# Another order of the work in a quantised feed-forward stage: marks behind products, down product three tiles behind, x standardised by ScalarE

## The reference, cut to what matters

```python
def fp4_quant_dequant(x):             # blocks of 16 along the last dim
    scale = max(max(|xb|) / 6, 1e-12)
    idx = searchsorted(MID, |xb / scale|)
    return GRID[idx] * sign(xb) * scale # grid 0 .5 1 1.5 2 3 4 6
def fp4_linear(x, w):
    return einsum('bsk,nk->bsn', quant(x), quant(w))
h = silu(fp4_linear(x, w_gate)) * fp4_linear(x, w_up)   # 256 -> 704
x = x + fp4_linear(h, w_down)                            # 704 -> 256
```

## Time and profile before

| | us |
|---|---|
| median of 3 runs | 4039.49 |
| profiled execution | 4052.42 |
| its span | 4050.6 |
| PE busy | 3277.3 (81%) |
| DVE busy | 2933.8 (72%) |
| ACT busy | 2218.7 (55%) |
| POOL busy | 1102.7 (27%) |

### The profile page before, as it was taken

The page is one execution under the profiler, slowest core; times in us unless marked ns, Lnnn a source line. Parts: engine busy times, 40 slices in busy tenths (PEclk is TensorE's granted clock), DMA queues, the critical chain, the costliest instruction groups (busy, mean ns, idle before and its releaser), DMA issues. The chain is left out here.

```text
span 4050.6 us, 80801 instructions
## 1 busy us (share of the span) xinstructions
PE 3277.3 (81%) x24792; PEld 2521.1 (62%) x24792; DVE 2933.8 (72%) x7319; ACT 2218.7 (55%) x5224; POOL 1102.7 (27%) x625
## 2 busy tenths in 40 slices
PE   6888887888879469899758888888888886498898
PEld 4666655665656358788635655565556654488787
DVE  4666665666657778888527788787877786589887
ACT  4656665666657323333227777777777775233332
POOL 1000000000000034555322333443334433354554
PEclk9988888899889789999868999899999997799999
DMA  4322323223232010000114334434443432100110
GB/s 82 55 41 37 52 37 52 43 41 48 37 53 32 22 42 16 16 16 16 61 31 63 53 62 67 72 54 65 67 66 59 67 54 46 67 25 27 31 31 26
DMA packets 131686, 185.58 MB, mean 46 GB/s; under 512 B 14102, under 2 KB 79766, under 8 KB 130838
## 3 DMA queue, kind: packets, MB, share of 16 engines
q1 hardware_dynamic: 131526, 183.90, 26.9%
HBM read 45.97 MB, written 28.84 MB: 18 GB/s over the span
## 5 line engine op out<-in xcount | busy, mean ns | idle before, releaser
L368 ACT ACTIVATE a_probs<-a_probs,a_negmax 128x128 f32<-128x128 f32 (+3 forms) x1024 | 569.1, 556 | 463.0 <-DVE a_negmax L291 462.9
L291 DVE CUSTOM_DVE_ANT_0 a_probs<-a_mask,a_score 128x128 f32<-128x128 f32 (+3 forms) x1024 | 487.0, 481 | 279.1 <-PE a_score L438 141.1
L446 PE MATMUL a_turned<-ident,a_probs 128*128 128x128 f32 x2560 | 487.9, 296 | 218.4 <-DVE a_pT L300 203.7
L446 PEld LDWEIGHTS a_turned<-ident,a_probs 128*128 128x128 f32 x2560 | 329.6, 149 | 314.7 <-DVE a_pT L300 213.1
L1023 PE MATMUL f_y_bank<-f_wdT,f_hqT 128*128 128x256 f32 x1536 | 389.0, 407 | 76.4 <-ACT f_hqT L961 76.4
L438 PE MATMUL a_score<-a_stack_k,a_stack_q 112*128 112x128 f32 (+3 forms) x1024 | 439.0, 441 | 0.9 <-DVE a_negmax L291 0.9
L1699 ACT ACTIVATE b_u<-b_u,b_negmax 128x512 f32<-128x512 f32 x512 | 366.5, 716 | 99.5 <-DVE b_negmax L1579 99.1
L1579 DVE CUSTOM_DVE_ANT_0 b_u<-b_u,b_score 128x512 f32<-128x512 f32 x512 | 340.4, 681 | 98.7 <-PE b_score L1825 97.0
L1834 PE MATMUL b_turned<-ident,b_u 128*128 128x128 f32 x2048 | 336.2, 291 | 67.8 <-DVE b_pT L1585 39.8
L1023 PEld LDWEIGHTS f_y_bank<-f_wdT,f_hqT 128*128 128x128 f32 x1536 | 307.3, 205 | 127.7 <-issue 80.9
L1571 DVE SCALAR_TENSOR_TENSOR b_u<-b_u,b_score 128x1024 f32<-128x1024 f32 x256 | 309.4, 1216 | 89.7 <-ACT b_u L1692 87.8
(11 more groups left out here) (224 smaller groups left out, 7042.6 us busy)
## 6 DMA issues: line engine op xcount, KB each, us to landing
b_stack<-b_part SPq DMA_DIRECT2D x192, 256.0 KB, 8.1
a_stack_q<-a_part SPq DMA_DIRECT2D x192, 128.0 KB, 4.5
a_stack_k<-a_part SPq DMA_DIRECT2D x192, 128.0 KB, 5.7
xs<-in_x_dram SPq DMA_DIRECT2D x16, 512.0 KB, 7.6
x_before_b<-xs SPq DMA_DIRECT2D x16, 512.0 KB, 2.9
b_xin<-x_before_b SPq DMA_DIRECT2D x16, 512.0 KB, 11.8
b_xres<-x_before_b SPq DMA_DIRECT2D x16, 512.0 KB, 3.8
x_after_b<-b_xres SPq DMA_DIRECT2D x16, 512.0 KB, 3.0
```

Of the source, the lines that this page charges most:

```text
L291: dve.tensor_tensor_reduce(out=probs[:, n % 2, j, 0:keys(n)], in0=mask_of(n), in1=score[j][:, 0:keys(n)], scale=-1.0, scalar=3.0e38, op0=A ...
L368: act.activation(probs[:, n % 2, j, 0:keys(n)], probs[:, n % 2, j, 0:keys(n)], ACT.Exp, bias=negmax[:, n, j:j + 1], scale=-1.0, accum_out= ...
L446: m = nc.tensor.transpose(turned[j % 2][:, u, :], probs[:, n % 2, j, u * P:(u + 1) * P], ident[:])
```

## The change

The marks of tile n-1 come behind the `hidden` steps of tile n in VectorE's queue. Transpose, hqT, down product and residual run three tiles behind instead of two. `xh` is made by ScalarE with an Identity activation (scale rstd, bias shift = -mean x rstd); VectorE makes -mean, POOL the product. The steps of the next sequence's x sit in other slots: statistics one sequence earlier (slot 3, for s + 2), standardising and scales in slot 0, `xu` at the end of slot 0, marks in slot 1, `xq` at the head of slot 2, the x transposes of the next sequence in slots 2 and 3, each low part at the head of the slot ahead of its tile. SyncE loads four sequences ahead. `nscale` has four buffers. The second to last sequence is written out too.

The core of the diff; semaphore counts that follow from it are left out:

```diff
-    LAG = 2
+    LAG = 3
...
+        nmean = sb("nmean", [P, TILES])
+        shift = sb("shift", [P, TILES])
...
-        nscale = sb("nscale", [P, 2, NB])
+        nscale = sb("nscale", [P, TILES, NB])
...
+            ahead = 4
             if x_from is not None:
-                load(0)
-                load(1)
-            with sp.Fori(0, SEQS - 2) as s:
+                for s in range(ahead):
+                    load(s)
+            with sp.Fori(0, SEQS - ahead) as s:
                 if x_from is not None:
-                    load(s + 2)
+                    load(s + ahead)
                 keep(s)
-            keep(SEQS - 2)
-            keep(SEQS - 1)
+            for s in range(SEQS - ahead, SEQS):
+                keep(s)
...
+                wait(pool, s_xh, TILES * s)
                 pool.tensor_tensor(out=rstd[:], in0=vare[:], in1=consts[:, 0:TILES], op=ALU.pow).then_inc(s_rstd, 1)
+                pool.wait_ge(s_rstd, 2 * s + 1)
+                pool.tensor_tensor(out=shift[:], in0=nmean[:], in1=rstd[:], op=ALU.mult).then_inc(s_rstd, 1)
...
+                                   in1=spread(nscale[:, t, :], NB), op=ALU.mult).then_inc(s_hq, 1)
+
+            def body(s):
+                for n, t, behind in slots(s):
+                    if n == 2 and has(s + 1):
+                        front_scale(s + 1)
                     if behind(1):
                         scale(*behind(1))
                     if t is not None:
                         divide(s, t)
-                    if n == 1 and not last:
+                    if n == 0 and has(s + 1):
                         front_divide(s + 1)
-                    if n == 2 and not last:
-                        front_scale(s + 1)
+                    if n == 3 and has(s + 2):
+                        front_norm(s + 2)
 
             front_norm(0)
             front_divide(0)
             front_scale(0)
+            front_norm(1)
...
+                wait(dve, s_rstd, 2 * s)
+                dve.tensor_scalar(out=nmean[:], in0=mv[:, :, 0], scalar1=-1.0, scalar2=None, op0=ALU.mult)
...
-                wait(dve, s_xu, s)
                 wait(dve, s_xq, s)
-                dve.wait_ge(s_rstd, s + 1)
-                for t in range(TILES):
-                    dve.tensor_scalar(out=xh[:, t * H:(t + 1) * H], in0=x_tile(xs, s, t), scalar1=mv[:, t, 0:1],
-                                      scalar2=rstd[:, t:t + 1], op0=ALU.subtract, op1=ALU.mult).then_inc(s_ln, 1)
-                dve.wait_ge(s_ln, s * LN + 3 * TILES)
+                dve.wait_ge(s_xh, TILES * s + TILES)
...
-                    dve.wait_ge(s_hq, T - 1)
+                    dve.wait_ge(s_hu, T - 1)
...
                 dve.wait_ge(s_mag, T + 1)
+                if not isinstance(T, int) or T >= 2:
+                    dve.wait_ge(s_hq, T - 1)
...
+                        front_low(s + (n + 1) // TILES if n == 3 else s, (n + 1) % TILES)
+                    if t is not None:
+                        hidden(s, t)
                     if behind(1):
                         round_hidden(*behind(1))
-                    if t is not None:
-                        hidden(s, t)
-                    if n == 2 and not last:
+                    if n == 0 and has(s + 1):
+                        front_scales(s + 1)
+                    if n == 1 and has(s + 1):
                         front_round(s + 1)
-                    if n == 3 and not last:
-                        front_low(s + 1, 0)
-                    if behind(2):
-                        residual(*behind(2))
-                    if n == 3 and not last:
-                        front_low(s + 1, 1)
-                    if n in (0, 1):
-                        front_low(s, n + 2)
-                    if n == 0 and not last:
-                        front_scales(s + 1)
+                    if behind(3):
+                        residual(*behind(3))
+                    if n == 3 and has(s + 2):
+                        front_norm(s + 2)
 
             front_norm(0)
             front_scales(0)
             front_round(0)
+            front_norm(1)
...
+            def front_standard(s):
+                act.wait_ge(s_rstd, 2 * s + 2)
+                wait(act, s_xu, s)
+                for t in range(TILES):
+                    act.activation(xh[:, t * H:(t + 1) * H], x_tile(xs, s, t), ACT.Identity, bias=shift[:, t:t + 1],
+                                   scale=rstd[:, t:t + 1]).then_inc(s_xh, 1)
...
+                        front_move(s + (n + 1) // TILES if n == 3 else s, (n + 1) % TILES)
                     if behind(1):
                         magnitude(*behind(1))
                     if t is not None:
                         do_silu(s, t)
-                    if n == 2 and not last:
+                    if behind(3):
+                        move_hidden(*behind(3))
+                    if n == 0 and has(s + 1):
+                        front_standard(s + 1)
+                    if n == 1 and has(s + 1):
                         front_mag(s + 1)
-                    if behind(2):
-                        move_hidden(*behind(2))
-                    if n == 3 and not last:
-                        front_move(s + 1, 0)
-                        front_move(s + 1, 1)
-                    if n in (0, 1):
-                        front_move(s, n + 2)
+
+            front_standard(0)
             front_mag(0)
             front_move(0, 0)
-            front_move(0, 1)
...
-                        turn_hidden(*behind(2))
+                    if behind(3):
+                        turn_hidden(*behind(3))
                     if t is not None:
                         expand(s, t, 1)
-                    if n == 3 and not last:
-                        front_turn(s + 1, 0)
-                    if behind(2):
-                        down(*behind(2))
-                    if n == 3 and not last:
-                        front_turn(s + 1, 1)
+                    if behind(3):
+                        down(*behind(3))
                     if n in (0, 1):
                         front_turn(s, n + 2)
+                    if n in (2, 3) and has(s + 1):
+                        front_turn(s + 1, n - 2)
```

More of the change, by code:

```diff
@@ L676, in ffn @@
         s_out = sem("x_stored")
-        s_steps = sem("loading_steps")
+        s_xh = sem("x_standardised")
         s_ln = sem("norm_steps")
@@ L712, in tile, with has, slots @@
             return s * TILES + t
+        def has(q):
+            return not isinstance(q, int) or q < SEQS
         def run(engine, body):
[L716 to L721, removed]
+            body(0)
+            with engine.Fori(1, SEQS - 2) as s:
+                body(s)
+            body(SEQS - 2)
+            body(SEQS - 1)
+        def slots(s):
+            first = isinstance(s, int) and s == 0
+            last = isinstance(s, int) and s == SEQS - 1
             for n in range(TILES + (LAG if last else 0)):
@@ L816, in _ @@
         def _(dve):
-            LN = 2 * TILES + TILES + 2
+            LN = 2 * TILES + 2
             def front_norm(s):
@@ L878, in hidden @@
                 dve.wait_ge(s_h, 2 * T + 1)
-                dve.tensor_scalar(out=nscale[:, i, :], in0=amax[:, i, :], scalar1=-SIXTH, scalar2=-SCALE_MIN,
+                dve.tensor_scalar(out=nscale[:, t, :], in0=amax[:, i, :], scalar1=-SIXTH, scalar2=-SCALE_MIN,
                                   op0=ALU.mult, op1=ALU.min)
@@ L900, in residual, with body @@
                                   op=ALU.add).then_inc(s_add, 1)
-            def body(s, first, last):
-                for n, t, behind in slots(s, first, last):
-                    if n == 0 and not last:
-                        front_norm(s + 1)
+            def body(s):
+                for n, t, behind in slots(s):
+                    if n < TILES and has(s + (n + 1) // TILES):
+                        front_low(s + (n + 1) // TILES if n == 3 else s, (n + 1) % TILES)
+                    if t is not None:
+                        hidden(s, t)
                     if behind(1):
                         round_hidden(*behind(1))
-                    if t is not None:
-                        hidden(s, t)
-                    if n == 2 and not last:
+                    if n == 0 and has(s + 1):
+                        front_scales(s + 1)
+                    if n == 1 and has(s + 1):
                         front_round(s + 1)
-                    if n == 3 and not last:
-                        front_low(s + 1, 0)
-                    if behind(2):
-                        residual(*behind(2))
-                    if n == 3 and not last:
-                        front_low(s + 1, 1)
-                    if n in (0, 1):
-                        front_low(s, n + 2)
-                    if n == 0 and not last:
-                        front_scales(s + 1)
+                    if behind(3):
+                        residual(*behind(3))
+                    if n == 3 and has(s + 2):
+                        front_norm(s + 2)
```

(2 more changed lines are left out.)

10 lines of the change are left out of this document (3 added, 7 removed).

## The result

The changed kernel takes 4348.63 us (median of 4 runs, 4328.84 to 4360.88), the kernel before 4038.97 beside it: ratio 1.0764, 95% interval 1.0718 to 1.0809, slower. The forecast was 4125 in a range of 4085 to 4170: right in sign, 224 us short. The profiled execution took 4360.88 (span 4359.1), against 4052.42 (4050.6).

The account below looks back on a forecast made before the run. Before, TensorE was taken to bound plain tiles (7.30 us), with x-work slots overrunning; after, a queue ring. Period 36.9 and c 62.9 gave stage 616.4, +42.5, twice +85: 4125 us, range 4085 to 4170.

Parts of the forecast that it names:

- the peeled body: Second to last sequence written out in the feed-forward: taken to cost 0, as no instruction is added.
- the other 2900: The us outside the two feed-forward stages, which the diff does not touch: claimed to stay as they are.
- The ring: Feed-forward tiles: a closed turn through VectorE, POOL and ScalarE queues, 8.77 us per tile, 35.08 per sequence; chance 0.82.
- One sign that the prediction named as being against it: Feed-forward slots: the forecast is wrong if `hid` waits for the up product instead.
- the clock term: Lag of three in the feed-forward: 0.4 us per sequence taken, of 0 to 1.3.
- Slot 1: Slot with the x marks, contending with POOL's `hq` and `hu`: +0.85 to +1.77 us, 1.3 taken.
- The ends: Stage is c + 15 periods: c = 62.9 us, with 23.0 before the first `hid` and 16.7 after the last.
- Costs at nothing: `xh` on ScalarE, `xq`, `xu`, SyncE's loads: 0; small nmean and shift steps: 0.3 us, lying in slot 3's waiting.
- 1: Rival: ring open at one link, above all `silu` not behind `mag`; TensorE bounds, period 29.2, 3891 us; chance 0.05.
- 2: Rival: the ring costs what each sequence loses today, so no change, period 34.1, 4040 us; chance 0.03.
- 3: Rival: the clock falls in every feed-forward slot, 4268 us with 1.3 us four times a sequence; chance 0.07.
- 4: Rival: Identity not in `silu`'s table, so two table loads per sequence, +38 us, 4163; chance 0.03.

Follow-up runs that it names:

- e1: Changed kernel with 50 empty semaphore increments behind the first feed-forward's VectorE stream; 4207.28 us, ratio 1.0414.
- e2: Kernel before with 57 empty semaphore increments behind the first feed-forward's VectorE stream; 4214.53 us, ratio 1.0428.
- e7: e1 with a second magnitude activation per tile, into a tile that nobody reads; 4271.78 us, ratio 1.0547.
- e4: e1 with VectorE's marks of a tile ahead of the next tile's hidden steps again; 4002.99 us, ratio 0.9894.
- e5: e1 with POOL's `hu` of tile n ahead of `hq` of tile n-1; 4029.76 us, ratio 0.9967.
- e6: e1 with ScalarE's order `silu`, `hqT`, `mag`; 3958.82 us, ratio 0.9796.
- e12: Changed kernel with 306 empty semaphore increments at the end of the first feed-forward's VectorE queue; 4209.77 us, ratio 1.0431.
- e11: Changed kernel with 256 empty semaphore increments at the end of the first feed-forward's VectorE queue; 4381.91 us, ratio 1.0858.

## Why the prediction was right and wrong

**The step that failed most is a zero.** "The four-wide nscale and the peeled body: 0, no instruction is added", and "the other 2900 stay as they are". The peeled body executes no instruction more, but it adds 57 to the stream, and they moved a loop to a place where it stalls: 160.1 us, over half of the loss and more than the whole forecast of 85. e1 and e2 show it, by taking the stall away and by bringing it into the kernel before. I counted instructions executed, not instructions laid out. The trace before held the warning: `a_pT` and `a_probs` idle for "issue" 13 times each, once a turn, in the first attention's loop, 129.7 us that the feed-forward's rows do not show and that the prediction did not look for.

**The ring: right.** 8.77 a tile was forecast from a different order's rows, 8.75 and 8.64 are measured, and the links come out one by one: 2.50, 0.86, 0.97, 1.36, 1.53, 0.70 and 0.83 in the first turn shown. Releasers as forecast: `hu` behind `hq` at 1.36, `silu` right behind `mag`, `hid` by `silu`. e7, e4 and e5 show it causally. One sign that the prediction named as being against it did come, in part: `hid` waits for the up product in one slot of four and now and then in a second (38 of 128 times, 139.0 us), and that is the clock term below.

**The period: two terms too small.** Slot 1: +1.3 taken of 0.85 to 1.77, measured 10.58 - 8.77 = +1.81, the upper end. VectorE does go between POOL's two operations; I took the middle. The clock: +0.4 taken of 0 to 1.3. The 1.3 is the 4.52 of the earlier trace rows less the 2.75 of the earlier trace rows, less the 0.4 to spare, rounded; no run shows the 0.4, which was my estimate. In its place the runs show 10.13 - 8.77 = +1.36 in the slot behind. The idle PE ahead of the down product comes in every sequence here, since slot 1 always makes it, so an average over sequences with a slow product and without was the wrong reading of the earlier trace rows. The four slots shown give 38.1, the mean over 14 periods is 38.42, against 36.9: +1.5, 15 times 23 us a stage. The high end, 38.3, was nearly the truth. What is between 38.1 and 38.42 is the clock too: in three of the 14 inner sequences of the first stage the down product of slot 0 is slow as well (4.08 to 4.34 us, granted clock 0.65 to 0.67) and that slot takes 10.0 to 10.2 instead of 8.7, and in two the product behind slot 1 takes 5.46 (granted clock 0.50) and its slot about 11.4.

**The ends: c is 646.9 - 15 x 38.42 = 70.6, not 62.9.** Before the first `hid` 24.05 (23.0 taken), and after the last `hid` 2075.22 - 2051.80 = 23.4 (16.7 taken). The last rows of the kernel after, first stage:

```profile
2060.65 5.04 PE L1039 MATMUL f_y_bank<-f_wdT,f_hqT 128*128 128x256 f32 x12 [4.61 <-ACT f_hqT L977]
...
2065.73 0.42 DVE L912 TENSOR_TENSOR xs<-f_y_bank,xs 128x256 f32<-128x256 f32 x1 [4.01 <-PE f_y_bank L1039]
...
2070.26 0.42 DVE L912 TENSOR_TENSOR xs<-f_y_bank,xs 128x256 f32<-128x256 f32 x1 [4.11 <-PE f_y_bank L1039]
...
2074.80 0.42 DVE L912 TENSOR_TENSOR xs<-f_y_bank,xs 128x256 f32<-128x256 f32 x1 [4.11 <-PE f_y_bank L1039]
```

With a lag of three, three tiles are left to turn, move and multiply when the last `hid` is done, one after another at 4.54 us, the first product in 5.04 at a granted clock of 0.55, the other two in 2.83 at 1.00. I had followed only the last tile's own path: its `hq` starts 10.06 behind `hid`, as forecast (10.02), but the rest takes 13.4, not 6.7.

**Costs at nothing.** `xh` on ScalarE, the small steps, `xq`, `xu` and SyncE: no releaser in the sequence shown is any of them. Eight of the 128 `hid` wait up to 2.5 us for "issue", 18.1 in all, which the kernel before has not; they cost nothing, since their slot, the one with the marks of x, takes 10.58 in the inner sequences with such a wait and without.

**Rivals.** 1 (TensorE bound, 3891) named the right link and missed the ring behind it: with `silu` alone 36.92, with `hqT` as well 31.34, still not 29.2, as the slots with x work stay longer than 7.30. Its condition, "if `silu`(n+1) did not queue behind `mag`(n)", was not enough. 2 fell. 3 (the clock in every slot, 4268 with 1.3 us four times a sequence) fell as such: one slot of four shows it in every sequence, a second one in a few. 4 (a table load for Identity) fell; the table loads of `silu`'s line after are as in the earlier trace rows, and `xh`'s line L945 has none:

```profile
L962 ACT ACT_TABLE_LOAD  x2: 1283/1283/1283, 1446.8 to 3723.4; - x2
```

The sum as it was: 42.5 + 15 x 1.5 + 7.7 = 72.7 for the first stage, measured 73.0; without the stall (e1) the kernel takes 4207, which is slower by 4.1% for the ring's reason, so the sign was not luck, but lies above the forecast's range too. So the stage's terms (slot 1, the clock, the ends) were 82 us short, and the zero some 141 to 160.

## What to carry to other kernels

When steps are set one tile later, write each engine's queue down and look for the closed turns: an operation that stands behind another tile's slow one can belong to a ring, and behind the first ring can stand a next one (here `silu`, then `hqT`, had to pass `mag`, worth 249 us against e1). A change to straight-line code moves every loop behind it (here 57 instructions, and 160.1 us with them): look at "issue" waits once per turn and at the instruction queue's packets in the whole trace, and try some empty steps ahead of the loop before judging an edit. A view of waits names the event that came last, not always one that was needed: read the code beside it (e6). A drain can grow with the lag (from the last `hid` to the end 13.65 us with a lag of two, 23.4 with three): the last tiles' steps come one after another.

## What the runs showed of the hardware

A loop of 302 VectorE instructions ran free or with 11.1 to 11.4 us of waiting per turn, by its place in VectorE's stream, and the same place came again after 256 instructions (0 and 256 added: stall; 50 and 306: none); nothing but the first instruction's idle time marked "issue" and the instruction queue's packets (118 in e1, 120 in e12, 177 after, 176 in e2, 179 in e11) tells of it. A loop of 392 stalled up to 6.5 and 4.4 us a turn in one place, 3.5 and 3.3 in another, and only 3.3 in a third; what sets those sizes, and whether its places repeat after 256 too, stays open. Where VectorE's mark of 1024 columns was asked for between two POOL operations of 704 that followed each other, the three ran in turn (recorded 2.24, 2.30 and 2.36 in a row, alone 1.39, 1.23 and 1.39). The down product behind 3.0 to 4.2 us of idle PE took 4.21 to 5.46 us in each of 28 sequences, at a granted clock of 0.50 to 0.67, instead of the 2.75 to 2.83 of the same product at 1.00.
